# Twelve tiles of the fullest expert computed inside phase one's drain, with a table that has a tile in each partition

## What is computed

```python
x = x + gnn(layernorm(x), adj, adj, Wq, Wk, Wv, Wo)   # 16 heads; softmax(q k / sqrt(512) + 2 adj) v, then Wo
x = x + ffn(layernorm(x), gate_W, gate_b, expert_W, expert_b)

def ffn(x, gate_W, gate_b, expert_W, expert_b):        # E, K = 8, 2
    scores = max(x @ gate_W + gate_b, 1e-4)
    p = softmax(scores); topk_idx = top_k(p, 2)
    w = max(p, 0.1); w = w / (sum of w over the two chosen)
    comb = w where chosen, else 0
    y = einsum('bsd,edf->bsef', x, expert_W) + expert_b
    return einsum('bsef,bse->bsf', y, comb) / K
```

## Time and profile before

| | us |
|---|---|
| median of 3 runs | 1673.04 (1672.6 to 1674.02) |
| profiled execution, its own time | 1672.73 |
| its span, first to last instruction | 1670.9 |
| PE busy | 1570.9 (94%) |
| DVE busy | 1194.8 (72%) |
| ACT busy | 988.1 (59%) |
| POOL busy | 974.0 (58%) |
| mean granted TensorE clock | 0.967 of full speed |

### The profile page before, as it was taken

One profiled execution on the slowest core, in us unless ns is written; L12 is line 12 of the kernel. 1 busy time (PEld: TensorE's weight loads), 2 busy tenths in 40 slices (PEclk: granted clock), 3 DMA queues, 4 the chain that ended last, 5 costly groups with the idle time before them and its releaser, 6 DMA issues. The chain is left out here.

```text
span 1670.9 us, 43148 instructions
## 1 busy us (share of the span) xinstructions
PE 1570.9 (94%) x11856; PEld 1370.9 (82%) x11856; DVE 1194.8 (72%) x4698; ACT 988.1 (59%) x3093; POOL 974.0 (58%) x1693
## 2 busy tenths in 40 slices
PE   6999999999999999999999999975289999999996
PEld 6899999899999999999999999964167777777774
DVE  5667888778887788878888788887535565555554
ACT  4787887778877788787887878775111111111111
POOL 3255665666656666566656666567335565665555
PEclk9999999999999999999999999977599999999998
DMA  7987787887878888887888878794548898898886
GB/s 232 235 222 221 226 253 227 255 247 225 257 228 253 240 226 251 233 240 222 232 240 235 241 220 227 217 287 138 212 95 165 166 171 161 166 169 161 160 162 104
DMA packets 188619, 351.84 MB, mean 211 GB/s; under 512 B 20960, under 2 KB 30304, under 8 KB 188256
## 3 DMA queue, kind: packets, MB, share of 16 engines
q1 hardware_dynamic: 135520, 238.47, 51.0%
q0 software_dynamic: 29680, 69.55, 21.7%
q10 hardware_dynamic: 23184, 41.05, 7.7%
HBM read 189.48 MB, written 159.52 MB: 209 GB/s over the span
## 5 line engine op out<-in xcount | busy, mean ns | idle before, releaser
L654 ACT ACTIVATE prob<-prob,nmax 128x128 f32<-128x128 f32 x1024 | 398.6, 393 | 164.3 <-DVE amax L803 151.8
L1060 POOL TENSOR_TENSOR prob<-prob,rinv 128x512 f32<-128x512 f32 x256 | 262.4, 1046 | 223.2 <-DVE rinv L820 222.9
L799 DVE CUSTOM_DVE_ANT_0 prob<-ps_s,bias 128x128 f32<-128x128 f32 x1024 | 237.7, 288 | 166.5 <-PE ps_s L516 129.1
L1258 POOL DMA_INDIRECT out<-yt,token x135 | 211.8, 1569 | 198.4 <-DMA out<-yt,token 81.8
L1196 ACT ACTIVATE xgT_hi<-ps_x 128x512 fp32r<-128x512 f32 x135 | 80.7, 598 | 387.8 <-PE ps_x L1181 318.1
L1175 PE MATMUL ps_y<-we,xgT_hi 128*128 x540 | 260.2, 482 | 7.5 <-DVE xgT_lo L1215 7.5
L1176 PE MATMUL ps_y<-we,xgT_hi 128*128 x540 | 214.3, 397 | 0.0
L1177 PE MATMUL ps_y<-we,xgT_lo 128*128 x540 | 213.5, 395 | 0.0
L654 ACT ACTIVATION_READ_ACCUMULATOR prob<-prob,nmax 128x1 f32 x1024 | 194.2, 190 | 0.0
L803 DVE TENSOR_REDUCE amax<-prob 128x4 f32<-128x512 f32 x256 | 175.7, 686 | 8.9
L1069 POOL DMA_INDIRECT x_lists<-xn,pos x128 | 135.6, 1059 | 66.1 <-DVE pos L924 37.8
(11 more groups left out here) (152 smaller groups left out, 4314.2 us busy)
## 6 DMA issues: line engine op xcount, KB each, us to landing
ks<-kq_parts SPq DMA_DIRECT2D x192, 256.0 KB, 4.2
qs<-kq_parts SPq DMA_DIRECT2D x192, 256.0 KB, 6.4
xg<-x_lists ACTq DMA_DIRECT2D x135, 260.5 KB
xin<-x SPq DMA_DIRECT2D x64, 256.0 KB, 7.0
kq_parts<-kT_hi SPq DMA_DIRECT2D x32, 512.0 KB, 3.9
kq_parts<-kT_lo SPq DMA_DIRECT2D x32, 512.0 KB, 5.0
kq_parts<-qT_hi SPq DMA_DIRECT2D x32, 512.0 KB
kq_parts<-qT_lo SPq DMA_DIRECT2D x32, 512.0 KB
```

The lines of the kernel that those rows point to most:

```text
L654: last = nc.scalar.activation(prob[:, r, c, h, :], prob[:, r, c, h, :], ACT.Exp, bias=nmax[:, r, i:i + 1], scale=-1.0, accum_out=rsum[:, r ...
L799: last = nc.vector.tensor_tensor_reduce(out=prob[:, r, c, h, :], in0=ps_s[c % 2][:, P * h:P * h + P], in1=bias[:, b % 4, :], scale=-1.0, s ...
L1060: tt(prob[:, r, q], prob[:, r, q], rinv[:, r, HC * q:HC * q + HC].unsqueeze(2).to_broadcast([P, HC, P]), ALU.mult)\
L1258: pool.indirect_dma_start(out=out, out_offset=bass.IndirectOffsetOnAxis(ap=token[:, m, :], axis=0), in_=yt[:, r, :], in_offset=None, compu ...
```

## The change

- DVE chooses, after the places of the first `KNOWN = 56` batches, the expert with most rows (`choose_early`, at (60, 3)), and an order of experts that has it first. SP loads experts in this order, so it stands in place 0 of `we`; its bias row goes to `b_first`.
- `FULL = 12` tiles of this expert go through PE in slots of steps 64 to 69: `T_AT` has the slots of their transposes, `Y_AT` those of their products, `ADD_AT` those of POOL's additions to `out`. They use a ring of five buffers (`AHEAD`); the first five loads are issued by ACT at (62, 2), the others by SP in steps 66, 67 and 69, each after the addition that empties its buffer. ACT multiplies with the token's weight as it reads the product, DVE adds bias times weight one slot later.
- Low parts of experts are all DVE's, in pieces of 512 columns: places 0 to 3 at `LO_AT`, 4 to 7 behind the whole loop. `HI_AT` has five slots changed.
- The table has a tile in each of 128 partitions and four columns (expert, row, count, place of the expert in `we`). DVE makes it at (68, 2), PE turns its columns into rows at (69, 0), DVE copies them behind the loop. A part that needs only the chosen expert is made at (64, 3) (`prepare_table`).
- PE's product for places moves from slot 0 to slot 1 of even steps, `scatter` from step 64 on stands in slot 3, padding is issued at (68, 2) by ACT and in step 69 by SP, before loads 9 to 11.
- Phase two has `LEFT = 123` tiles. Several buffers stand in another order in memory, so that early tiles take the room of dead ones.

```diff
-        tab = sb(top, "tab", [1, 3, TILES], i32)
+        tab = sb(top, "tab", [1, 4, P], i32)
...
+        T_AT = {(64, 1): 0, (64, 3): 1, (65, 1): 2, (65, 3): 3, (66, 1): 4, (67, 2): 5, (67, 3): 6, (68, 2): 7, (68, 3): 8, (69, 0): 9, (69, 1): 10, (69, 2): 11}
+        Y_AT = {(64, 3): 0, (65, 1): 1, (65, 3): 2, (66, 1): 3, (67, 2): 4, (67, 3): 5, (68, 2): 6, (68, 3): 7, (69, 0): 8, (69, 1): 9, (69, 2): 10, (69, 3): 11}
+        ADD_AT = {(65, 1): 0, (66, 1): 1, (66, 2): 2, (67, 0): 3, (68, 0): 4, (68, 1): 5, (69, 0): 6, (69, 1): 7, (69, 2): 8, (69, 3): 9, (70, 0): 10, (70, 1): 11}
+        LOAD_AT, LOADS_SP = (62, 2), {66: (5, 6), 67: (7, 8), 69: (9, 10, 11)}
...
+        def early_load(queue, j):
+            m = j % AHEAD
+            if j == 0:
+                queue.wait_ge(rows_done, 1)
+                queue.wait_ge(X_full, B)
+                for k in range(4):
+                    queue.wait_ge(scattered[k], 32 * (KNOWN // 4))
+            if j >= AHEAD:
+                queue.wait_ge(rows_done, 1)
+                queue.wait_ge(added_e[m], 16 * (j // AHEAD))
+            row = queue.value_load(early_i[0:1, j:j + 1], min_val=0, max_val=ROWS - P)
+            queue.dma_start(xg_e[:, m, :], x_lists[bass.ds(row, P), :]).then_inc(xg_e_in[m], 16)
...
+        def early_hi(act, j):
+            act.wait_ge(xgT_e_full, j + 1)
+            if j == 0:
+                act.wait_ge(pT_full, DC * (B - 1))
+            if j >= 2:
+                act.wait_ge(y_e_full, j - 1)
+            nc.scalar.activation(xgT_e_hi[:, j % 2].rearrange("p c t -> p (c t)"), ps_m[:, :], ACT.Copy).then_inc(xgT_e_hi_done, 1)
+
+        def early_lo(dve, j):
+            m = j % AHEAD
+            dve.wait_ge(xgT_e_hi_done, j + 1)
...
+        def early_out(act, which, j, bank):
+            act.wait_ge(y_e_full, j + 1)
+            nc.scalar.activation(xg_e[:, j % AHEAD, 0:D], bank, ACT.Identity, bias=zero_col[:, :], scale=weight(which, j)).then_inc(y_e_read, 1)
...
-        HI_AT = [(B - 2, 1), (B - 2, 2), (B - 1, 1), (B - 1, 2), (B, 2), (B + 1, 0), (B + 1, 2), (B + 2, 3)]
-        LO_AT = {0: (B - 2, 3), 2: (B - 1, 3), 4: (B, 3), 5: (B + 1, 2), 6: (B + 2, 0), 7: (B + 3, 0)}
-        POOL_LO_AT = {1: (B - 2, 3), 3: (B - 1, 3)}
+        HI_AT = [(B - 2, 1), (B - 2, 3), (B - 1, 1), (B - 1, 2), (B, 2), (B + 1, 3), (B + 3, 0), (B + 3, 1)]
+        LO_AT = {0: (B, 0), 1: (B, 2), 2: (B + 1, 0), 3: (B + 2, 0)}
...
                 if t == B - 3:
+                    hold(order_done, 1)
                     hold(V_full, B)
...
+                    if (t, c) == (B + 5, 0):
+                        pe.wait_ge(cols_done, 1)
+                        pe.wait_ge(pT_done, DC * B)
+                        for i in range(4):
+                            last = nc.tensor.transpose(ps_t[0:1, P * i:P * i + P], choice[:, 10, i:i + 1], ident)
+                        last.then_inc(cols_full, 1)
...
-                    if c == 0 and t % 2 == 0 and okp(p):
+                    if c == 1 and t % 2 == 0 and okp(p):
                         pe.wait_ge(route_step, ROUTE * p + 15)
...
+                    if (t, c) == LOAD_AT:
+                        act.wait_ge(order_done, 1)
+                        first_expert.append(act.value_load(order_i[0:1, 0:1], min_val=0, max_val=E - 1))
+                        for j in range(AHEAD):
+                            early_load(act, j)
...
+                    if (t, c) == (KNOWN + 4, 3):
+                        choose_early()
+                    if (t, c) == (B, 3):
+                        prepare_table()
...
+            dve.wait_ge(cols_full, 1)
+            nc.vector.tensor_copy(tab[:, :, :].rearrange("p r t -> p (r t)"), ps_t[0:1, :]).then_inc(tab_step, 1)
+            for e in range(len(LO_AT), E):
+                expert_lo(e)
...
-                    if c == 3 - 2 * a and okp(p):
+                    if c == (3 - 2 * a if t < B else 3) and okp(p) and (p, a) != (B // 2 - 1, 1):
                         scatter(p, a)
+                        if p == B // 2 - 1:
+                            scatter(p, 1)
...
-            return Item(g, N, off, TILES)
+            return Item(g, N, off, LEFT)
```

More of the change, by code:

```diff
@@ L750, in constants_out, with table, link, total @@
                 nc.vector.tensor_copy(zero_tile[:, D:D + 1], const[:, C_DUM:C_DUM + 1]).then_inc(consts_done, 1)
+                nc.vector.memset(zero_col[:, :], 0.0).then_inc(row_done, 1)
+                dve.wait_ge(row_done, 1)
+                nc.vector.tensor_copy(place_i[:, :], zero_col[0:1, :]).then_inc(row_done, 1)
+            iota = const[:, C_TILE:C_TILE + E]
+            over = lambda column: column.to_broadcast([P, E])
+            def table():
+                dve.wait_ge(place_step, PLACE * (B // 2))
+                nc.vector.tensor_copy(ends[:, :], fill[0:1, 0, :]).then_inc(fill_done, 1)
+                dve.wait_ge(pT_full, DC * B)
+                more = prob[:, 1, 0].rearrange("p h m -> p (h m)").rearrange("p (e b) -> p e b", e=E)
+                one, n_e, past, skip, passed, part, sums = (prob[:, 1, 1, 0, E * i:E * i + E] for i in range(7))
+                cols = choice[:, 10, :]
+                row = const[:, C_ROW:C_ROW + 1]
+                step = [0]
+                def link(ins):
+                    step[0] += 1
+                    ins.then_inc(tab_step, 1)
+                    dve.wait_ge(tab_step, step[0])
+                def total(out_, in_):
+                    return nc.vector.tensor_reduce(out_, in_, axis=AX.X, op=ALU.add)
+                link(nc.vector.memset(one, 1.0))
+                link(tt(n_e, fill[:, 0, :], const[:, C_BASE:C_BASE + E], ALU.subtract))
+                link(tt(more, n_e.unsqueeze(2).to_broadcast([P, E, B]), const[:, C_MULT:C_MULT + B].unsqueeze(1).to_broadcast([P, E, B]), ALU.is_gt))
+                link(total(n_e, more))
+                link(tt(n_e, n_e, taken, ALU.subtract))
+                link(nc.vector.tensor_tensor_scan(past, one, n_e, 0.0, ALU.mult, ALU.add))
+                link(nc.vector.scalar_tensor_tensor(out=skip, in0=n_e, scalar=-float(P), in1=skip_more, op0=ALU.mult, op1=ALU.add))
+                link(tt(passed, past, over(row), ALU.is_le))
+                link(total(cols[:, 0:1], passed))
+                link(tt(part, passed, skip, ALU.mult))
+                link(total(cols[:, 1:2], part))
+                link(tt(part, passed, d_slot, ALU.mult))
+                link(total(cols[:, 3:4], part))
+                link(tt(part, past, over(row), ALU.is_lt))
+                link(total(sums[:, 0:1], part))
+                link(tt(cols[:, 1:2], cols[:, 1:2], row_base, ALU.add))
+                link(tt(cols[:, 3:4], cols[:, 3:4], slot[:, 0:1], ALU.add))
+                link(tt(cols[:, 2:3], cols[:, 0:1], sums[:, 0:1], ALU.not_equal))
+                dve.wait_ge(dep_in, 16)
+                link(tt(cols[:, 2:3], cols[:, 2:3], dep[:, :], ALU.add))
+                link(ts(cols[:, 2:3], cols[:, 2:3], 16.0, None, ALU.mult))
+                ts(cols[:, 0:1], cols[:, 0:1], float(E - 1), None, ALU.min).then_inc(cols_done, 1)
@@ L780, in low_part_of_x @@
                 unit = small(t, c)
+                if unit and unit[0] == "T":
+                    early_lo(dve, unit[1])
                 if not unit or unit[0] != "X":
@@ L971, in _ @@
                             choose(p)
-            dve.wait_ge(place_step, PLACE * (B // 2))
-            nc.vector.tensor_copy(ends[:, :], fill[0:1, 0, :]).then_inc(fill_done, 1)
-            dve.wait_ge(pT_full, DC * B)
-            free = prob[0:1].rearrange("p a c h m -> p (a c h m)")
-            one, n_e, past, skip = (free[:, E * i:E * i + E] for i in range(4))
-            passed, more = (free[:, at_:at_ + a * b].rearrange("p (a b) -> p a b", a=a) for at_, a, b in ((4 * E, TILES, E), (4 * E + TILES * E, E, B)))
```

257 lines of the change are left out of this document (193 added, 64 removed).

## The result

| | before | after |
|---|---|---|
| median of 5 runs | 1672.60 us (1669.79 to 1674.02) | 1679.96 us (1673.15 to 1680.50) |
| ratio to before | | 1.0039, 95% interval 1.0022 to 1.0057 |
| profiled execution | 1672.73 us, span 1670.9 | 1673.15 us, span 1671.4 |

The change makes the kernel **0.39% slower**, where 0.8% faster was predicted; the time lies outside the range. The balance of gains and losses is made with that trace.

A forecast was written before the change was run, and what follows sets the result against it. Phase one's drain was taken as bound by its dependency chain, not PE's work. Phase two gives back 38.9 us, the drain grows by 28: 1672.7 - 38.9 + 28 = 1661.8, less 2 for overlaps, 1660 us; range 1643 to 1675.

The forecast's parts named there:

- Term 5: Behind the last places: the table, a low part and the last four early tiles' products, which end at about 1215.
- Term 6: End of the drain: VectorE's 16 subtraction pieces take 9.6 us, hiding only the last addition of 0.8 + 4.9 us.
- term 4: DMA queue before the last places: the fifth early load waits behind the biases, delaying scores and choice; +4 us net.
- the 2 us taken off for overlaps: In the sum: waits assumed to add at two early loads may overlap instead, worth 0 to 4 us.
- (b): Drain, table as short rows on 128 partitions: 5.7 us after the last places instead of 9.5.
- near or after 1181: Sign in the drain: the last pair's scores begin then, behind a low part that waits for an early load.
- under 0.7: Sign over steps 65 to 69: a granted clock below this would mean the rival of a slow clock.
- slower by the clock: Rival, chance 0.14: the drain's clock stays low, twelve tiles cost 72 us instead of 39, total 1677 us.
- The drain hides them well: Rival, chance 0.2: PE's idle time in the drain takes most early tiles, drain +13 us, total 1647 us.
- (a): Drain, steps 62 and 63: subtractions leave, the choice comes first, about 6 of PE's 8.4 us wait go.
- no change: Rival, chance 0.07: the five buffers' turns delay the last addition to 1230 to 1235; drain +38, total 1672 us.
- the rule of the ring: DMA queue: one issuing engine's descriptors go in order, so the fifth early load lands after 1176.3, behind the biases.

The follow-up runs named there:

- again: The changed kernel run once more without any edit, giving a second trace of it: 1678.29 us, ratio 1.0039 to before.
- the one wait added: Against the changed kernel, the end subtractions stay last but wait until GpSimd has issued the last addition: 1670.34 us, ratio 0.9990.
- mended_seven_again: Second run, seven early tiles, subtractions in VectorE's waits, SyncE's paddings behind its last early load, list writes' old slot, later roundings, against the changed kernel: 1656.41 us, ratio 0.9909.
- gaps: Against the changed kernel, the four experts' end subtractions moved into stretches where VectorE waits for early tiles: 1669.82 us, ratio 0.9985.

## Why the prediction was wrong

It had the sign wrong, and the time by 18 to 20 us. Almost all of that lies in three terms of the drain. By its own count, from the start of the span, phase two's first product was to come 28 us later and came 46.8 us later in `again`: 13.3 of the 18.8 us missing lie behind the last places (terms 5 and 6, 13.8 by the first execution, from which the lengths below are taken) and 5.5 ahead of them (term 4; 2.0 in the first execution). Phase two gave 2.4 us more than predicted, and the 2 us taken off for overlaps were not found.

**What held.** Phase two: twelve tiles gave 41.3 us, 38.9 were predicted (what follows its first product, 462.7 us for 135 tiles, is 3.43 us a tile, not 3.24). The table, (b): from the last places to its last column 1198.61 + 0.15 - 1193.36 = 5.4 us, 5.7 predicted. The subtractions' own length: 9.70, 9.6 predicted. The change of phases: 9.58, 9.6. The order of the low parts ahead of the scores and the choice: in the first execution the scores began at 1181.45, "near or after 1181" predicted. The clock: 0.82 from the gate product of step 65 to 1228 in `again`, where under 0.7 was the rival's sign, and twelve tiles added 82.2 - 37.6 = 44.7 us of PE's work and not 72. So the rival "slower by the clock" is refuted, though its direction came true. "The drain hides them well" is refuted as well.

**Of (a)** the wait went whole (8.44 us to none, "1 to 3" predicted), but the 6 us were no gain: the gate product of step 65 came 32.5 us after that of step 63, 32.3 before.

**Term 6 failed**, by 6.6 us. "Nothing hides them but the last addition" laid 0.8 + 4.9 us of addition beneath 9.6 of subtractions. From their start to phase two's first product 19.2 us were predicted and 25.8 passed, since the addition came behind them. A row of before spoke against it: in the earlier trace rows a subtraction of 2.29 us lasted 5.67 beside GpSimd's of 4.51. That row was used for (a), and not for the very engine pair of term 6. The edits show the cause of the loss: with the one wait added, 8.2 us are gone. The Trainium skill's "SBUF — State Buffer" (SBUF: two separate sides) says that a VectorE instruction with two SBUF inputs and a GpSimd instruction that reads SBUF share a port pair, that whichever starts first has it for the whole instruction, and that the other fully blocks. The trace agrees that GpSimd is blocked, but not for how long: the cast stood 10.71 us, across sixteen instructions of 0.67 us, and in `mended_seven_again` sixteen such instructions blocked neither a cast nor an issue. So why GpSimd was held for the whole run stays open.

**Term 5 failed**, by 7.2 us. From the last places to the start of the subtractions 25.6 us were predicted; 32.8 passed. It counted load 11 as the late one and had tile 8's products start 6.4 us after the last places. They started after 16.7 us, behind tile 9's transposes and so behind load 9. From there to the subtractions 16.1 us passed where 19.2 were predicted. The paddings that delayed load 9 stood only in the rival "no change", at 4.6 us and on SyncE. Moved, SyncE's four and ScalarE's four give 6.7 us together.

**Term 4 failed in its cause**, and in size by 5.5 us (+4 for the last places predicted, +9.5 in `again`; +6.0 in the first execution). It was right in that low parts stand ahead of scores and choice, and wrong in what they wait for. The biases landed as before:

```profile
e_bias<-expert_b SPq DMA_DIRECT2D x1, 2048.0 KB, 11.2
```

but tile 5 didn't wait for a load, so the rule of the ring cited there isn't what set this time, and no run shows whether it holds. In its place stood two roundings on ScalarE and the wait for list writes, of which the text had no term: the scatter's move was described, its buffer's next writer was not asked for. Both undone give 4.7 of the front's 11.7 us in the trace, and 1.3 us of time, within the error. The other 7.0 us, 5.0 of them between the gate product of step 67 and the last places, were not taken apart.

**The range.** It took in each mechanism alone, with the slower side given to the clock only. No rival had two engines' work laid side by side and found in a row. Two of its sums don't close: its own bounds (5 + 8 up, 4 + 6 down from 1660) give 1650 to 1673, not 1648 to 1670, and the shares of its cases give 0.11 within 0.2% and 0.14 slower, not 0.09 and 0.16. Neither would have saved it.

**Do the gains add?** 9.0 (gaps), 6.7 (paddings) and 1.3 (front) would be 17.0; together they gave 14.2 and, the second time, 15.9, which is as much within the error. The first two alone gave 11.2 of 15.7.

**Open.** What holds GpSimd behind the loop and not inside it. Why seven tiles beat twelve by more in time (5.3 us) than the tails and phase two of the traces account for (0.4 and 1.4). The spans of the profiled executions differ by 1.9 us only, but the twelve's was 2.8 us below its median and the seven's 0.7 above. The profiled run was the shortest of its set for the change and five of the fifteen runs, where luck would give about three in all; whether that is more than luck isn't known. The 2.2 us before gate product 63 were not tried alone.

## What to carry to other kernels

Filling an idle TensorE pays only as long as a tile adds less behind the last input than it saves later; count that for each tile. Of the two numbers tried here, seven was better than twelve. Before a run of VectorE instructions with two SBUF inputs goes beneath an addition of GpSimd's, ask whether GpSimd still has to issue it; if so, let it issue first, or take the run away from the end, and look in the trace whether it is still held. And a DMA moved into a busy stretch is priced by what stands behind it in its queue and behind that in PE's order, not by its own length.

## What the runs showed that was not expected

- A run of sixteen VectorE subtractions behind the loop let no GpSimd instruction in between, though each is only 0.67 us long. A cast of 128x1 took 10.71 (0.79 otherwise), an indirect DMA's issue 10.75 (1.57 otherwise). The same sixteen inside the loop held neither (0.75 and 1.75), while groups of four there held a cast for 2.83 us and, in part, an issue for 3.05.
- A wait removed in a trace need not be a time gained: two edits with stretches 4.5 and 3.2 us shorter than `again` in the trace left the ratio where it was.
